# A hybrid attention and feed-forward layer on one core: the table of slots that orders all engines' work is given new numbers in each of its six classes

## The reference, cut to what matters

```python
x = x + attn_a(layernorm(x), W_dq, W_uq, W_dkv, W_uk, W_uv, W_o)
x = x + ffn(layernorm(x), W_r, W_k, W_v, mu_r, mu_k)
x = x + attn_b(layernorm(x), Wq, Wk, Wv, Wo)
x = x + ffn(layernorm(x), W_r, W_k, W_v, mu_r, mu_k)

# attn_a: 16 heads, causal, keys and values from one latent c_kv of 64 columns
c_kv  = x @ W_dkv.T
q_lat = einsum('bqhd,hdl->bhql', q, k_eff)
attn  = softmax(where(causal, einsum('bhql,bkl->bhqk', q_lat, c_kv) / sqrt(8), -inf))
y     = einsum('bhql,hld->bqhd', einsum('bhqk,bkl->bhql', attn, c_kv), v_eff)

# attn_b: 16 heads of 8 columns, causal, q and k scaled to unit length
sim = einsum('bhid,bhjd->bhij', l2norm(q), l2norm(k)) * 8
out = (softmax(where(causal, sim, -max)) @ v) @ Wo

# ffn: xr, xk mix a row with the row before it
out = sigmoid(xr @ W_r) * (square(relu(xk @ W_k)) @ W_v)
```

## Time and profile before

| what | value |
|---|---|
| time, median of 3 runs | 1086.67 us (1085.28 to 1087.6) |
| the profiled execution: its own time | 1086.84 us |
| its span, first to last instruction | 1085.1 us |
| mean granted clock of TensorE | 0.946 of full |
| TensorE busy | 948.4 us, 87% |
| VectorE busy | 876.0 us, 81% |
| ScalarE busy | 768.9 us, 71% |
| GpSimd busy | 282.1 us, 26% |

### The profile page before, as it was taken

How to read it: one execution, slowest core, us unless ns; L and a number is a source line. 1 busy time by engine, 2 the same in 40 slices (tenths; PEclk the granted TensorE clock), 3 DMA queues, 4 the chain that set the end, 5 groups by cost and what they waited for, 6 DMA issues and landing times.

```text
span 1085.1 us, 37311 instructions
## 1 busy us (share of the span) xinstructions
PE 948.4 (87%) x15889; PEld 519.7 (48%) x15889; DVE 876.0 (81%) x2112; ACT 768.9 (71%) x1042; POOL 282.1 (26%) x264
## 2 busy tenths in 40 slices
PE   3688889799889899999989899999989899898794
PEld 1334445354455455454545455454545545454352
DVE  3978978888788898989898988889888987764633
ACT  2165677577757778887878777787868777788681
POOL 6111213123122232223223232323222231223212
PEclk8599989899989999999999999999999999899897
DMA  5244433346327162633627180624527180504130
GB/s 146 71 105 101 119 95 80 89 114 176 82 73 184 35 173 53 165 94 104 154 69 188 36 211 19 189 64 120 139 82 176 36 211 3 129 3 127 60 70 19
DMA packets 94342, 112.95 MB, mean 104 GB/s; under 512 B 15200, under 2 KB 81888, under 8 KB 94176
## 3 DMA queue, kind: packets, MB, share of 16 engines
q1 hardware_dynamic: 94176, 110.56, 39.3%
...
HBM read 55.22 MB, written 54.53 MB: 101 GB/s over the span
## 4 chain that ended last, share of the span: by engine, by line
PE 58%; DVE 23%; ACT 12%; issue 4%; POOL 2%; DMA 1%; SPq 0%; POOLq 0%; DVEq 0%; ACTq 0%
PE acc L729 20%; PE pool L712 10%; DVE rowmax L1081 9%; ACT prob L930 7%; PE pool L595 5%; PE pool L643 5%; PE pool L762 3%; PE pool L609 3%; PE pool L770 3%; PE pool L659 3%; PE pool L784 2%; ACT vals_a L916 2%; DVE xn L1039 2%; PE pool L802 1%; ACT vals_b L916 1%
## 5 line engine op out<-in xcount | busy, mean ns | idle before, releaser
L930 ACT ACTIVATE prob<-pool 128x1024 f32<-128x1024 f32 x576 | 568.1, 1031 | 137.1 <-PE pool L659 133.4
L1081 DVE TENSOR_REDUCE rowmax<-pool 128x2 f32<-128x1024 f32 (+7 forms) x480 | 357.3, 790 | 59.8 <-PE pool L659 57.2
L729 PE MATMUL acc<-prob,vals_b 128*32 128x512 f32 (+7 forms) x2048 | 170.3, 431 | 1.9 <-issue 0.8
L729 PE MATMUL acc<-prob,vals_a 128*32 128x64 f32 (+7 forms) x2048 | 168.8, 420 | 0.2 <-ACT prob L930 0.2
L643 PE MATMUL pool<-stack_ka,stack_qa 48*64 48x512 bf16 (+7 forms) x2048 | 121.0, 304 | 47.8 <-ACT vals_a L916 15.9
L712 PE MATMUL pool<-stack_qa,stack_ka 51*64 51x512 bf16 (+7 forms) x2048 | 110.5, 296 | 24.0 <-DVE rowmax L1081 12.2
L659 PE MATMUL pool<-mask_t,ident_b 64*64 64x128 bf16 (+1 forms) x2304 | 130.1, 216 | 0.0
L712 PE MATMUL pool<-stack_qb,stack_kb 48*64 48x512 bf16 (+7 forms) x2048 | 114.2, 302 | 9.0 <-DVE rowmax L1081 4.8
L1292 POOL TENSOR_TENSOR rstd<-mv,minus_half 128x4 f32<-128x4 f32 x64 | 65.1, 1018 | 154.5 <-DVE mv L1034 154.5
L643 PEld LDWEIGHTS pool<-stack_ka,stack_qa 48*64 48x64 bf16 x2048 | 43.2, 108 | 128.5 <-issue 65.7
L1304 POOL TENSOR_TENSOR parts_q<-rest_q,parts_q 128x512 bf16<-128x512 f32 x32 | 37.5, 1171 | 176.6 <-DVE parts_q L1055 176.4
...
## 6 DMA issues: line engine op xcount, KB each, us to landing
...
```

Of the source, the lines that this page charges most:

```text
L729: last = eng.matmul(acc[32 * j:32 * j + 32, BLK * blk:T], vals[a][:, blk, GROUP * g + j, :], prob[n % NPROB][:, k, at:at + T - BLK * blk], ...
L930: eng.activation(prob[n % NPROB][:, :, :], place["unit", n][0][:, :, :], ACT.Exp, scale=scale).then_inc(S["exped"], 1)
L1081: last = eng.tensor_reduce(to, of, axis=AX.X, op=ALU.max)
```

## The change

Only numbers in `PLANS` change. Every class gets new slots; the same steps with the same instructions are issued, and all line numbers stay. The diff of class `None`:

```diff
     None: {
-        "load": [-124.6],
-        "prepare_front": [-117, -106.5, -100.2, -95, -90.3],
-        "restack_a": [-102.4, -88.1],
-        "row_maxima0": [-64, -60, -55, -51, -47.7, -46, -44.2, -35.5, -35.2],
-        "max_rows0": [-31.5, -22.5],
-        "row_maxima1": [-33, -32.5, -25.5, -20, -15.7, -14.2, -9.2, -7, -6],
-        "max_rows1": [0.5, 2.5],
-        "values_a": [-34.8, -34.5],
-        "half_norm": [30],
-        "middle_front": [37, 39.7, 45, 47.5, 57.5, 57.8, 62, 65, 68.5, 71],
-        "restack_b": [90.6, 103.6],
-        "middle_back": [73, 80, 85, 90, 90, 93, 94, 98, 105, 109, 113],
-        "values_b": [-35.2, -34.6],
+        "load": [-146.7],
+        "prepare_front": [-118, -106.5, -100.7, -95, -90.3],
+        "restack_a": [-93, -57.1],
+        "row_maxima0": [-64, -60, -55, -51, -48.2, -45, -43.2, -35.5, -35.2],
+        "max_rows0": [-26.7, -22.6],
+        "row_maxima1": [-33.3, -32.5, -25.8, -20.5, -15.7, -13.7, -9.2, -6, -6],
+        "max_rows1": [-1.7, 2.2],
+        "values_a": [-35.3, -35.2],
+        "half_norm": [29.9],
+        "middle_front": [37, 38.7, 45, 48, 57.5, 58.5, 62.3, 65, 70, 70.8],
+        "restack_b": [81.3, 92.5],
+        "middle_back": [74, 80, 85, 90, 90, 92.5, 94, 98, 106, 110, 113],
+        "values_b": [-34.6, -34.5],
         "half_norm_b": [22.4],
-        "finish": [33.5, 35.2, 38.2, 40.2, 44.2, 48.7, 53.2, 54, 57, 57, 62.7, 77.2],
+        "finish": [34.5, 35.2, 38.2, 40.5, 44.2, 48.7, 53.2, 53.7, 57, 57, 63.2, 71.5],
```

More of the change, by code:

```diff
@@ new lines @@
+        "prepare_front": [-112.5, -107.8, -106, -106, -100.3],
+        "restack_a": [-51.1, -48],
+        "row_maxima0": [-71.4, -58.5, -49.5, -46.8, -44.9, -40.9, -38.9, -38.2, -38],
+        "max_rows0": [-23.8, -18.5],
+        "row_maxima1": [-34.2, -32, -19.7, -16.5, -15.5, -9.9, -9.5, -7.5, -7.5],
+        "max_rows1": [-2, 6],
+        "values_a": [-28.6, -24.8],
+        "half_norm": [23.8],
+        "middle_front": [33, 36, 38, 43, 47, 52.7, 53, 55, 58, 64.2],
+        "restack_b": [106.9, 113.2],
@@ new lines @@
+        "max_rows1": [0.2, 4.2],
+        "values_a": [-35.7, -5.3],
+        "half_norm": [26.1],
+        "middle_front": [36.7, 38.2, 43.7, 51.2, 55.9, 57.8, 59.2, 62, 63.3, 69.3],
+        "restack_b": [123.5, 135.2],
+        "middle_back": [77.7, 86, 93, 96, 96, 98.5, 102.5, 103.5, 111, 115.3, 119],
+        "values_b": [-31.3, -29.7],
+        "half_norm_b": [26.1],
+        "finish": [41.2, 43.7, 45, 48, 51.7, 54.7, 59.7, 61.2, 62.2, 64.2, 66.7, 73.5],
+    },
+    2: {
+        "load": [-100],
+        "prepare_front": [-66.5, -57.5, -55, -53, -49.8],
+        "restack_a": [-69.7, -66.7],
+        "row_maxima0": [-31.2, -26.5, -24.2, -23.2, -20.3, -20, -20, -17, -16.5],
+        "max_rows0": [-11.5, -8.5],
+        "row_maxima1": [-15.5, -14, -13, -12.3, -12, -9.5, -9, -4.2, -2.5],
+        "max_rows1": [7.3, 7.5],
+        "values_a": [-65.7, -36.8],
+        "half_norm": [29.7],
+        "middle_front": [33.5, 35, 39.3, 43.3, 50.3, 55.3, 57.5, 65, 69, 72],
+        "restack_b": [97.6, 123.5],
+        "middle_back": [72, 79, 85.3, 90, 90, 91, 94, 97, 106.6, 110.3, 112.3],
+        "values_b": [-42, -37.2],
+        "half_norm_b": [29.3],
+        "finish": [33, 34.5, 37, 39, 43, 47, 52.3, 53, 54, 56.3, 59.3, 72.3],
@@ L115 @@
[L115 to L118 removed]
+        "load": [-127.7],
+        "prepare_front": [-116, -107.5, -105, -102.5, -89.8],
+        "restack_a": [-94.2, -93.9],
+        "row_maxima0": [-59.7, -57.7, -56.5, -51, -51, -47.5, -44.5, -37.5, -36],
+        "max_rows0": [-25.5, -12],
+        "row_maxima1": [-32.8, -32.5, -25.5, -19.5, -17.5, -16.5, -10.5, -9.5, -7.5],
@@ L119 @@
+        "max_rows1": [1, 3.3],
+        "values_a": [-51.1, -47],
+        "half_norm": [24.7],
+        "middle_front": [35.3, 37.3, 46, 48.3, 51, 53.7, 56.7, 64, 66, 73],
+        "restack_b": [109, 145.3],
+        "middle_back": [77.3, 83.3, 85.8, 88.3, 91, 93, 93, 96.7, 99.7, 108.3, 109],
+        "values_b": [-58.5, -46.5],
+        "half_norm_b": [19.1],
+        "finish": [36, 36.3, 38, 47.7, 48, 49.5, 53.5, 57, 58.8, 61.8, 66.5, 66.7],
     },
     -1: {
-        "load": [-153.7],
-        "prepare_front": [-114.8, -107.5, -101, -91, -89],
@@ L136 @@
+        "values_a": [-55.5, -38.4],
+        "half_norm": [30.9],
+        "middle_front": [40, 49.7, 50.7, 53, 53.8, 58.4, 58.4, 59.7, 60.2, 65.2],
+        "restack_b": [73.6, 123.7],
+        "middle_back": [72.6, 73.3, 76.3, 76.8, 80.3, 81.3, 81.5, 82.6, 83.3, 85.3, 85.3],
+        "values_b": [-47.9, -11.3],
+        "half_norm_b": [25.4],
+        "finish": [38.4, 44, 44.5, 47, 49, 50.7, 58, 60.7, 62, 64, 64.3, 64.7],
     },
```

89 lines of the change are left out of this document (17 added, 72 removed).

## The result

The changed kernel takes 1047.48 us (median of 4 runs, 1046.14 to 1052.68), the kernel before 1085.97 (4 runs, 1082.57 to 1087.6). The ratio is 0.964, with a 95% interval of 0.9614 to 0.9667. The forecast was 1069 with a range of 1056 to 1088: the sign was right, the gain of 38 us was twice the 18 forecast, and the time lies outside the range.

What follows compares the result with a forecast made beforehand. No single engine was the bound: VectorE bounds the b half, TensorE the a half, with slack at the ends. Terms -2.8 - 5.2 + 0 - 5.2 - 1.0 - 3.4 = -17.6 from 1086.84 gave 1069 us, range 1056 to 1088.

Steps and rivals of the forecast that it cites:

- VectorE early in the b half: Repeated turns: xn escapes GpSimd's parts_q but still meets x_a; -0.4 us a turn, -2.8 in seven, bounds 0 and -9.5.
- TensorE's wait and the clock: Repeated turns: the 1.65 us wait for vals_a is cut up, fewer half-clock stretches follow; -5.2 us, bounds 0 and -9.0.
- `mparts` at the end of the b half: Repeated turns: mparts avoids GpSimd's x_ffn, but yT ends later and statistics wait; 0, bounds -0.7 and +0.9 us a turn.
- the slower rival: Repeated turns: wo late in each, a long clock fall following every time; 1095 us, chance 0.14.
- Head: Up to 373.5 us: three waits of VectorE and TensorE shorten, together -5.2 us.
- the first (-1.2): Head, at 61.32 us: VectorE's 3.36 us wait for row maxima shortens as batch 1's split of k passes two; -1.2 us.
- The second: Head, at 102.08 us: TensorE's 2.60 us wait for an xn shortens as it passes row maxima; -1.5 us.
- The third: Head, at 206.56 us: TensorE's 5.44 us wait for mparts shortens, mparts preceding statistics; -2.5 us, bounds 0 and -5.4.
- Late turns: Turns of batches 14 and 15: same pattern as the repeated turns with other numbers; -1.0 us, bounds 0 and -2.4.
- End: Last stretch: batch 15's q and k chain starts earlier, -2.5 us; y_b avoids GpSimd's x_out, -0.9; together -3.4.
- All falls go, and TensorE's waits shrink too: Rival: no clock falls in the middle, VectorE's idle time there also shrinks, ends gain as forecast; 1058 us, chance 0.08.
- the main case: Whole kernel: the terms as summed to 1069 us, own range 1059 to 1078 with terms halved or at one and a half; chance 0.55.

Runs made afterwards that it cites:

- splitq: Kernel before, with only the split of q one slot later in class None (batches 3 to 13): 1084.04 us, ratio 0.9954.
- pair: Kernel before, with values_a at its new slots and the split of q one slot later, both in class None: 1071.96 us, ratio 0.9858.
- xa_first: Changed kernel, with one number of class None moved so GpSimd issues x_a ahead of parts_q, directly behind its y_a: 1051.39 us, ratio 0.967.
- values_back: Changed kernel, with values_a of class None back at its old slots: 1058.59 us, ratio 0.9734.
- ends_only: Changed kernel with class None back at its old numbers, so only classes 0, 1, 2, -2 and -1 are new: 1081.11 us, ratio 0.9926.
- values: Kernel before, with only the two slots of values_a in class None changed to the new ones: 1097.7 us, ratio 1.0076.
- none_only: Kernel before, with the new numbers in class None alone (batches 3 to 13): 1074.16 us, ratio 0.9883.
- maxrows_back: Changed kernel, with max_rows1 of class None back at its old slots, so mparts stand behind yT again: 1052.69 us, ratio 0.9681.
- five: Changed kernel, but class None has its old numbers except five: values_a, the split of q and max_rows1 are new. 1048.54 us, ratio 0.964.
- after_again: The changed kernel itself, unchanged, measured and profiled once more: 1046.63 us, ratio 0.9614.
- tail_back: Changed kernel, with classes -2 and -1 (batches 14 and 15) back at their old numbers: 1056.74 us, ratio 0.9676.
- class0_back: Changed kernel, with class 0 (batch 0) back at its old numbers: 1046.98 us, ratio 0.9604.
- class1_back: Changed kernel, with class 1 (batch 1) back at its old numbers: 1052.29 us, ratio 0.9658.
- class2_back: Changed kernel, with class 2 (batch 2) back at its old numbers: 1053.04 us, ratio 0.966.

## Why the prediction was off, point by point

By the spans, 39.3 us were gained where 17.6 were forecast. Of the 21.7 us between them, 7.7 lie in the repeated turns (15.7 for 8.0), 8.9 in the head (14.1 for 5.2) and 6.9 in the late turns (7.9 for 1.0); the end gave 1.8 less. Two steps of the prediction failed above all: in the repeated turns "VectorE is busy 96% of this half, and sets its length", by which TensorE's wait was priced at nothing, and outside them the place early in the b half had hardly a term.

**VectorE early in the b half: -2.8 forecast.** The step that failed here is "`xn` still stands directly behind `y_a`, which releases `x_a`: GpSimd starts it while the first `xn` runs". The collision as such is real, and costs what was said: with `x_a` issued there, four `xn` take 2.11 us. But `x_a` is queued behind `parts_q` on GpSimd, whose cast comes after `xn` in the new order. It started 3.9 us after its `y_a`. The order of GpSimd's queue was to be read, and was not. The Trainium skill's page "SBUF — State Buffer", section "Who interferes with whom", has the one of the two operations that comes later wait for the other's end; the collision measured here agrees (2.11 us for four `xn`, 1.10 without it). Which operations meet is a matter of this kernel's queues.

**The part that had no term.** The forecast said of TensorE's wait for `vals_a`: "I expect no time from the wait itself: VectorE is busy 96% of this half, and sets its length." `splitq` shows that VectorE alone doesn't: with `xn` free at 1.11 us, the half stayed at 28.7. With both edits it takes 27.75 (`pair`). Put back alone in the changed kernel, the collision makes it 28.4 (`xa_first`) and the old slots of the values 28.8 (`values_back`), against 27.9. What fits all of these is two paths of nearly the same length, one through VectorE's `xn` and one through the copies `vals_a`; that reading is argued, since each edit also changes who waits for whom. Like with like, b6 and a9 took 58.8 us before, 57.8 in `pair` and 57.6 in the changed kernel. At 1.2 us a turn that is an estimated 8.2 in seven turns (1.17 each), where I had 2.8.

**TensorE's wait and the clock: -5.2 forecast, -9.0 measured.** "Cut into pieces below 1.65 us, they should let part of the falls go" was the right mechanism with too small a size: all five falls went. Each count of falls here is of one execution. The waits at this place, counted over the profiled executions: 1.65 us, five falls in seven turns (before) and four (`ends_only`); 2.75 us, five (`values`); 1.38 us, one (`splitq`) and two (`values_back`); 0.97 us, none in `pair`, `none_only`, `xa_first`, `maxrows_back`, `five`, `after_again`, `tail_back`, `class0_back`, `class1_back` and the changed kernel. In `class2_back` one short fall began at 682.9 us, right behind another wait, of 1.77 us and without a releaser in the profile; one of 1.57 us in `pair` had no fall behind it. That the length of the one wait counts, and not the idle time in sum, is borne out by `splitq` and `values_back` alone: TensorE idles 2.4 us in an undisturbed b half of theirs, as before, and there were one and two falls instead of five. 422.0 - 9.0 - 8.2 would be 404.8; the turns take 406.3, and b7, with a wait of 1.32 us without a releaser, is 1.3 longer than its like.

**`mparts` at the end of the b half: 0 forecast.** Right for the repeated turns, with both of its parts as they were described: 0.91 us became 0.14, and the statistics wait 0.82 us for `x_ffn`. `maxrows_back` leaves the a half as it is. `wo` was not late, so the slower rival has no case.

**Head: -5.2 forecast, -14.1 measured.** Of the three terms, the first (-1.2) was wrong: VectorE's wait grew, from 3.36 to 3.92, and a0 took 87.7 us instead of 86.7; why was not separated. The second was right for the wait, 2.60 to 1.03 for a forecast of 1.5; its half a1 took 2.0 us less in one profile of the changed kernel and 0.3 more in the other. The third, -2.5, was mis-sized: the wait fell by 5.1 us, and with it back at 3.81 (`maxrows_back`) the half is 5.9 us longer. What had no term at all is that the place early in the b half recurs in b1 and b2, which the cut into "seven repeated turns" hid: these halves went from 31.3 and 32.9 us to 27.9 and 29.1, -7.2 together. The half b0 gave another 3.5 (38.4 to 34.9), of which the old class 1 takes 2.5 back; it had no term either.

**Late turns: -1.0 forecast, -7.9 measured.** The same omission: the old waits for `vals_a` stood in b10 and b11 too, and in b12 a fall of 6.8 us (936.5 us on) with a half of 32.2 us, now 28.8. Putting batches 14 and 15 back costs it all (157.8), as does the old class `None` (158.1), so both are needed; of class `None` the five numbers are enough (149.9). Which step of batches 14 and 15 carries it was not separated.

**End: -3.4 forecast, -1.6 measured.** Batch 15's chain did start earlier in the list, but the wait for its q and k is 4.46 us, not 2.4. The step "This chain starts two to three slots earlier, a slot being 59.0 / 72 = 0.8 us: -2.5 of it" took slots for time, and the upper end of them. TensorE's place in the list moved with it, and what it waits for is still `qk`; why it is no shorter was not separated. By halves, b13 takes 1.8 us more than before, b14 and b15 2.9 and 1.2 less. The collision at `y_b` did go: 0.42 us instead of 1.32.

**The rivals.** "All falls go, and TensorE's waits shrink too", 1058 us at 0.08, was the nearest. It had the middle nearly right (its terms there add up to -19.5, measured -15.7) and both ends too small. One sum is slightly off: the main case with its terms at one and a half gives 1060 us, not 1059.
